# Third layer's edges: the last column of each half found by one-hot products in place of a gather

## The reference

```python
q = ((src @ q_w.T + q_b) * scaling).reshape(n, H, HD)
k = (src @ k_w.T).reshape(n, H, HD)
v = (src @ v_w.T).reshape(n, H, HD)
w = jnp.einsum('ehd,ehd->eh', q[e_dst], k[e_src])
mx = jax.ops.segment_max(w, e_dst, num_segments=n)
ex = jnp.exp(w - mx[e_dst])
den = jax.ops.segment_sum(ex, e_dst, num_segments=n)
attn_w = ex / (den[e_dst] + 1e-16)
agg = jax.ops.segment_sum(attn_w[:, :, None] * v[e_src], e_dst, num_segments=n)
x = _batchnorm(src + agg.reshape(n, D) @ out_w.T + out_b, g1, b1)
```

## Time and profile before

| | |
|---|---|
| time, median of 3 runs | 4790.94 us (4788.01 to 4792.92) |
| the profiled execution's own time | 4801.15 us |
| its span, first to last instruction | 4799.3 us |
| busy: DVE / POOL / ACT / PE | 3583.7 / 3313.6 / 2745.0 / 2121.5 us |
| mean granted TensorE clock | 0.736 |
| `layer2_edges` | about 2741 to 3752 us of the span |

### The profile page before, as it was taken

How to read it: one execution, slowest core, us unless ns; L and a number is a source line. 1 busy time by engine, 2 the same in 40 slices (tenths; PEclk the granted TensorE clock), 3 DMA queues, 4 the chain that set the end, 5 groups by cost and what they waited for, 6 DMA issues and landing times. The chain is left out here.

```text
span 4799.3 us, 60694 instructions
## 1 busy us (share of the span) xinstructions
PE 2121.5 (44%) x11977; PEld 1206.2 (25%) x11977; DVE 3583.7 (75%) x7007; ACT 2745.0 (57%) x6085; POOL 3313.6 (69%) x2937
## 2 busy tenths in 40 slices
PE   4499999999853000000000400000000458889995
PEld 3255554444422000000000200000000235555553
DVE  9365665555547899999997588888988657777776
ACT  0388888788722888888884322232222245655663
POOL 0488888888726777777772477777777337777774
PEclk9799999999976555555555755555555679999998
DMA  9655555555633577777674456666666323333332
GB/s 401 207 101 101 105 107 95 97 100 101 129 70 131 212 261 269 270 258 277 255 275 192 141 186 218 217 211 210 217 219 210 97 70 118 118 115 117 126 120 85
DMA packets 281953, 816.71 MB, mean 170 GB/s; under 512 B 62437, under 2 KB 177653, under 8 KB 269554
## 3 DMA queue, kind: packets, MB, share of 16 engines
q1 hardware_dynamic: 102828, 561.89, 31.0%
q0 software_dynamic: 169776, 248.56, 23.7%
q10 hardware_dynamic: 9238, 5.24, 0.5%
HBM read 366.96 MB, written 448.51 MB: 170 GB/s over the span
## 5 line engine op out<-in xcount | busy, mean ns | idle before, releaser
L643 POOL DMA_INDIRECT tab<-arena x560 | 952.4, 1701 | 210.3 <-issue 132.2
L1576 PE MATMUL psum<-ident,arena 128*128 128x128 f32 x15 | 3.7, 428 | 2145.9 <-DVEq L1604 2145.9
L773 PE MATMUL psum<-arena 128*128 128x512 bf16 (+1 forms) x4704 | 949.7, 357 | 0.0
L1948 POOL DMA_INDIRECT arena<-table,arena x784 | 748.1, 954 | 242.4 <-issue 238.5
L2448 POOL DMA_INDIRECT arena<-table,arena x622 | 630.1, 1013 | 191.3 <-issue 179.8
L1331 POOL DMA_INDIRECT arena<-table,arena x588 | 610.2, 1038 | 179.3 <-issue 172.3
L2530 PE MATMUL psum<-arena 128*128 (+1 forms) x4050 | 685.5, 332 | 90.6 <-DVE arena L2578 49.6
L773 PEld LDWEIGHTS psum<-arena 128*128 128x128 bf16 x4704 | 433.7, 99 | 473.6 <-issue 24.6
L1576 PEld LDWEIGHTS psum<-ident,arena 128*128 128x128 f32 x15 | 2.7, 214 | 2146.4 <-DVEq L1604 2146.2
L2530 PEld LDWEIGHTS psum<-arena 128*128 (+1 forms) x4050 | 402.0, 99 | 366.6 <-issue 115.8
L1379 ACT ACTIVATE arena<-arena 128x128 f32<-128x128 f32 x1344 | 408.8, 387 | 92.1 <-DVE arena L1498 88.5
(11 more groups left out here) (426 smaller groups left out, 5164.9 us busy)
## 6 DMA issues: line engine op xcount, KB each, us to landing
rows<-arena SPq DMA_DIRECT2D x56, 3808.0 KB
arena<-seg_rows SPq DMA_DIRECT2D x112, 896.0 KB, 7.1
rows<-arena SPq DMA_DIRECT2D x56, 1008.0 KB, 4.7
seg_rows<-arena SPq DMA_DIRECT2D x28, 1792.0 KB
rows<-arena SPq DMA_DIRECT2D x56, 896.0 KB, 3.9
arena<-table,arena POOLq DMA_INDIRECT x1994
arena<-src_lanes SPq DMA_DIRECT2D x56, 448.0 KB
tab<-arena POOLq DMA_INDIRECT x560
```

The costliest lines, as they stand in the source:

```text
L643: eng.indirect_dma_start(out=m.tabs[j], out_offset=bass.IndirectOffsetOnAxis(ap=idx[g][:, k:k + 1], axis=0), in_=rows[g][:, k, 0:D], in_of ...
L773: t = eng.matmul(ps[:, c, 0:w], part[n // 2 % PAIRS][:, n % 2, :], hot[n % HOTS][:, lo:lo + w], start=False, stop=False, skip_group_check= ...
L1948: eng.indirect_dma_start(out=kv[k][:, j, :], out_offset=None, in_=m.table2, in_offset=bass.IndirectOffsetOnAxis(ap=idx[k][:, j:j + 1], axi ...
```

## The change

For all but the first four halves, the 14th column is no longer gathered. `layer2_edges` loads `table2` into SBUF once and splits it into three bf16 parts (`part_cols`; the third lies in `xN`'s memory). For each half, SP loads keys to all partitions (index minus block start, for 25 blocks by 128 lanes), ScalarE turns them into the one-hot `hot` (Abs, then Relu), TensorE adds 25 blocks x 3 parts = 75 products of 256 columns into `found`, and ScalarE copies that to the place where the gather would have put it. To make room, queries have two buffers, the marks over all features one, and small tiles lie in weights already used. Since `xN` is overwritten, `layer2_nodes` adds the input on TensorE from `xT` by products with the identity, and VectorE only copies.

```diff
+HALVES = T // HALF
+SIX = 6
 def layer2_edges(nc, m, I):
-        q = [A(HALF, D) for _ in range(RING)]
+        q = [A(HALF, D) for _ in range(2)]
...
+        part_cols = [A(NB * 2 * D, dt=BF16) for _ in range(2)] + [m.xN[:, :, :].rearrange("p b f -> p (b f)").bitcast(BF16)]
+        hot = A(NB * P, dt=BF16)
+        KEYS = [(0, 13), (13, NB)]
+        found = m.psum[:, 2, 0:2 * D]
+        tab = [kv[3 - c].rearrange("p t f -> p (t f)")[:, 0:(b - a) * 2 * D] for c, (a, b) in enumerate(KEYS)]
-        all_keeps = [A(D, COLS) for _ in range(2)]
+        all_keeps = A(D, COLS)
...
             @block.sync
-                def turn(i, last):
+                def load_keys(at):
+                    for c, (a, b) in enumerate(KEYS):
+                        eng.dma_start(keys[c], m.keys2[at, a * P:b * P].rearrange("t l -> (t l)").partition_broadcast(P)).then_inc(keys_in, 16)
+                def turn(i, first, last):
                     for k in range(RING):
                         hold(eng, in_psum, i * RING + k + 1)
-                        if k == 0 or not last:
-                            load(i, k + RING - 1)
+                        if k < 2 or not last:
+                            load(i, k + 2)
+                        if (k >= 2 or not first) and (k < 1 or not last):
+                            hold(eng, apart, 2 * (nth(i, k) - 1))
+                            load_keys(bass.ds(i * RING + k + 3, 1))
                         hold(eng, sums_made, nth(i, k) + 2)
...
+                for c, (a, b) in enumerate(KEYS):
+                    eng.dma_start(tab[c].rearrange("p (b f) -> p b f", f=2 * D), m.table2.rearrange("(b p) f -> p b f", p=P)[:, a:b, :]).then_inc(tab_in[c], 16)
+                for k in range(2):
                     load(0, k)
+                eng.dma_start(lanes_found[0:HALVES, :], m.src_lanes[0:T, :].rearrange("(n t) l -> n t l", t=HALF)[:, HALF - 1, :]).then_inc(lanes_in, 16)
+                eng.wait_ge(keys_made, 1)
+                eng.dma_start(m.keys2, hot.bitcast(F16)[0:HALVES, :]).then_inc(keys_stored, 16)
...
             @block.gpsimd
-                with eng.Fori(0, LOOPS) as i:
+                gather(0, HALF)
+                with eng.Fori(1, LOOPS) as i:
+                    gather(i, HALF - 1)
+            @block.tensor
+            def _(eng):
+                def block_sums(g, n, first=False, last=False):
+                    for p, part in enumerate(part_cols):
+                        t = eng.matmul(found, hot[:, bass.ds(g * (SIX * P) + n * P, P)], part[:, bass.ds(g * (SIX * 2 * D) + n * 2 * D, 2 * D)],
+                                       start=(first and p == 0), stop=(last and n == SIX and p == 2))
+                    return t
+                eng.wait_ge(low_made, 2)
+                with eng.Fori(1, HALVES - RING + 1) as n:
+                    hold(eng, hot_made, n)
+                    block_sums(0, 0, first=True)
+                    with eng.Fori(0, (NB - 1) // SIX - 1) as g:
+                        for b in range(SIX):
+                            block_sums(g, 1 + b)
+                    for b in range(SIX):
+                        t = block_sums((NB - 1) // SIX - 1, 1 + b, last=True)
+                    t.then_inc(found_made, 1)
             @block.scalar
...
+                def one_hots(i, k):
+                    eng.wait_ge(keys_in, 32 * (nth(i, k) - 3))
+                    for c, (a, b) in enumerate(KEYS):
+                        eng.activation(hot[:, a * P:b * P], keys[c], ACT.Abs, bias=lane_ids[:, 0:1]).then_inc(apart, 1)
+                    eng.wait_ge(apart, 2 * (nth(i, k) - 3))
+                    eng.activation(hot, hot, ACT.Relu, bias=m.ones[:, 0:1], scale=-1.0).then_inc(hot_made, 1)
+                def keep_found(i, k):
+                    eng.wait_ge(found_made, nth(i, k) - 3)
+                    eng.wait_ge(free[k], i + 1)
+                    eng.activation(kv[k][:, HALF - 1, :], found, ACT.Copy).then_inc(found_in, 1)
...
                         hold(eng, scores_made, nth(i, k) + 2)
                         eng.activation(ex[h], gap[h], ACT.Exp, scale=-1.0).then_inc(exped, 1)
-                        stage_marks(k, edges(i, k + 2))
+                        if (k >= 3 or not first) and (k < 3 or not last):
+                            keep_found(*half(i, k + 1))
+                        stage_marks(k + 1, edges(i, k + 1))
                         if k + 1 < RING or not last:
                             keep_query(*half(i, k + 1), by_edge[:, HALF, :])
...
                         eng.activation(rows[h][:, :, MAX:R2], top[h][:, :, 1:COLS].rearrange("p a t -> p t a"), ACT.Copy).then_inc(filled, 1)
+                        if (k >= 2 or not first) and (k < 2 or not last):
+                            one_hots(*half(i, k + 2))
...
             @block.vector
                     elif step == 1:
-                        eng.wait_ge(landed[k], 16 * HALF * (i + 1))
+                        eng.wait_ge(landed[k], 16 * ((HALF - 1) * i + HALF))
+                        eng.wait_ge(found_in, nth(i, k) + 1)
...
+                eng.tensor_tensor(hot.bitcast(F16)[0:HALVES, :].rearrange("p (b l) -> p b l", l=P), spread(lanes_found[0:HALVES, :], 1, [HALVES, NB, P]),
+                                  spread(block_at[0:HALVES, :], 2, [HALVES, NB, P]), ALU.subtract).then_inc(keys_made, 1)
...
+                eng.wait_ge(low_made, 2)
+                for k in range(2, RING):
+                    eng.engine_nop().then_inc(free[k], 1)
                 for step in range(SCORES2):
                     score(0, 0, step)
...
 # layer2_nodes
-                        t = eng.transpose(ps[:, 6 + k % 2, n * P:(n + 1) * P], sT[:, b * P:(b + 1) * P], m.ident[:, :])
+                        to = ps[:, 6 + k % 2, n * P:(n + 1) * P]
+                        eng.matmul(to, sT[:, b * P:(b + 1) * P], m.ident[:, :], start=True, stop=False)
+                        t = eng.matmul(to, m.xT[:, b * P:(b + 1) * P], m.ident[:, :], start=False, stop=True)
...
-                    eng.tensor_tensor(y[:, b0:b1, :], ps[:, 6 + k % 2, 0:CHUNKS[k][1]].rearrange("p (b f) -> p b f", f=D), m.xN[:, b0:b1, :], ALU.add).then_inc(y_made, 1)
+                    eng.tensor_copy(y[:, b0:b1, :], ps[:, 6 + k % 2, 0:CHUNKS[k][1]].rearrange("p (b f) -> p b f", f=D)).then_inc(y_made, 1)
```

More of the change, by code:

```diff
@@ L1867 @@
 SUMS2 = OLD2 + HALF
+HALVES = T // HALF
+SIX = 6
+assert (NB - 1) % SIX == 0
 def layer2_edges(nc, m, I):
@@ L1884, in layer2_edges @@
         old = A(D + H2)
-        all_keeps = [A(D, COLS) for _ in range(2)]
+        all_keeps = A(D, COLS)
         keeps = [A(HALF) for _ in range(2)]
-        resets = [A(H2 * COLS + 1) for _ in range(2)]
+        resets = [used_up[:, 6 * H2 * COLS + h * (H2 * COLS + 1):6 * H2 * COLS + (h + 1) * (H2 * COLS + 1)] for h in range(2)]
         idx = [A(HALF, dt=I32) for _ in range(RING)]
         SUM, MAX = D, D + H2
-        q_first, q_in = sem("first_queries_landed"), [sem(f"queries_landed{k}") for k in range(RING)]
+        q_first, q_in = sem("first_queries_landed"), [sem(f"queries_landed{k}") for k in range(2)]
+        ids_made, lanes_in, keys_made, keys_stored = sem("block_ids_made"), sem("found_lanes_landed"), sem("keys_made"), sem("keys_stored")
+        keys_in, apart, hot_made = sem("keys_landed"), sem("keys_apart"), sem("one_hots_made")
+        found_made, found_in = sem("rows_found"), sem("found_rows_kept")
+        tab_in = [sem(f"table_landed{c}") for c in range(2)]
+        high_made, rest_made, mid_made, low_made = sem("high_parts"), sem("rests"), sem("middle_parts"), sem("low_parts")
         begun = sem("buffers_begun")
@@ L1946, in _ @@
                         hold(eng, free[k], i + 1)
-                        for j in range(HALF):
+                        for j in range(n):
                             eng.indirect_dma_start(out=kv[k][:, j, :], out_offset=None, in_=m.table2,
                                                    in_offset=bass.IndirectOffsetOnAxis(ap=idx[k][:, j:j + 1], axis=0)).then_inc(landed[k], 16)
+                gather(0, HALF)
[18 more added lines that the diff above has]
+                    t.then_inc(found_made, 1)
             @block.scalar
@@ L1955, in stage_marks @@
                                    spread(m.reset[:, at], 1, [P, H2, HALF]), ACT.Copy).then_inc(marks, 1)
-                    eng.activation(all_keeps[k % 2][:, :, 1:COLS], spread(m.keep[:, at], 1, [P, D, HALF]), ACT.Copy).then_inc(marks, 1)
+                    eng.activation(all_keeps[:, :, 1:COLS], spread(m.keep[:, at], 1, [P, D, HALF]), ACT.Copy).then_inc(marks, 1)
                 for k in range(RING):
@@ L1962, in keep_query @@
                     eng.activation(by_edge[:, 0, :], before, ACT.Copy).then_inc(last_kept, 1)
-                    eng.wait_ge(q_in[k], 16 * i + 16)
+                    eng.wait_ge(q_in[k % 2], 16 * (i * (RING // 2) + k // 2 + 1))
                     eng.wait_ge(last_kept, i * RING + k + 1)
```

(39 more changed lines are left out.)

40 lines of the change are left out of this document (30 added, 10 removed).

## The result

The changed kernel takes 5047.26 us, median of 4 runs (5032.8 to 5051.13), beside 4789.48 for the kernel before on the same chip (4 runs, 4786.49 to 4792.92). The ratio is 1.0532, 95% interval 1.051 to 1.0555: 5.3% slower. The forecast was 5201 with a range from 5000 to 5330; the direction and the place are right, the size is 154 us too large.

A forecast was written before the change was run, and what follows sets the result against it. POOL's gathers were taken to bound the third layer's edges, VectorE close behind. Start +16, first halves -2 and 52 slower halves +396 gave +410 us on the span; forecast median 5201 us, range 5000 to 5330.

The forecast's parts named there:

- What bounded the kernel, and what the gather was worth: Third layer's edges: POOL's gathers pace a half at 17.64 us; one gather fewer leaves VectorE's ring of 16.59.
- The new ring, without VectorE: Third layer's edges: found rows' copy 0.37, marks to state columns 4.49, one-hots 6.1, hand-overs 0.3, then TensorE's products.
- 11.26 + X: Cost in us of a half in the third layer's edges once X is over about 6; forecast 25.3.
- X: Time of TensorE's 75 products for a half in the third layer's edges, forecast at 14.0 us.
- Four register operations a block: TensorE's sequencer, loop over blocks: four address operations a block, 0.131 us apart; three turns take 11.4 us.
- The rival of the array: TensorE's array sets the products' pace, register operations hidden: X = 10.7, 22.0 us a half, 5030 us; 22%.
- The clock stays low: Rival: TensorE's product bursts never get the high clock: X = 16.0 + 0.3, 27.6 us a half, 5321 us; 15%.
- A reload in each ring: Rival: ScalarE reloads its table between exponentials and one-hots, +1.28 us in each of 52 halves: 5268 us; 5%.
- Products hidden: Rival: TensorE's products fit their gap, X at 6.0 or less, a half 16.95 us: 4769 us, faster; 4%.
- The start: Third layer's edges, up to the first exponential: table, lanes, keys and parts come first, 46.2 us for 30.3, +16.
- The first three halves: Halves at the start of the third layer's edges, forecast to gain 3 x 0.69 = 2.1 us.
- The nodes: Third layer's nodes: 25 more TensorE products run beside VectorE, whose additions become copies: 0 to +2 us, taken as 0.

The follow-up runs named there:

- Kernel 8: The kernel before with 13 gathers a half from the fifth on and nothing in the 14th's place: 4736.15 us, ratio 0.9898.
- kernel 1: The changed kernel with only the table's high part multiplied, 25 products a half: 6287.23 us on the first chip, 4765.66 us on another (ratio 0.9967).
- kernel 6: The changed kernel with one-hots made one half earlier and found rows in two PSUM banks, nothing left out: 4794.92 us, ratio 1.0018.
- kernel 9: The changed kernel with one-hots a half earlier, found rows' copy behind the state columns, blocks written out, one-hots' first 13 blocks released early: 4758.89 us, ratio 0.9954.
- kernel 2: The changed kernel with the loop's turns written out, no register arithmetic between products: 5990.85 us on the first chip, ratio 1.0256, distorted by pauses.
- kernel 3: The changed kernel with 82 (first 88) unread products behind each burst to keep the clock high: run again, 5030.9 us, ratio 1.0533.
- kernel 4: The changed kernel with turns written out and unread products added behind each burst (82 when run again): 4952.22 us, ratio 1.0364.

## Why the prediction came out as it did

- **What bounded the kernel, and what the gather was worth: right.** POOL's pace, with VectorE's ring close behind. Kernel 8 measures 48 us in all, where 1.05 us a half was forecast: 0.86 came.
- **The new ring, without VectorE: right, and shown.** The ring of `keep_found`, state columns, one-hots and products holds when taken apart at either end: fewer products (kernel 1) or one half of distance (kernel 6) and the wait is gone. Its ScalarE link was 10.9 us where 10.96 and hand-overs were forecast, and a half follows 11.26 + X: 22.4 by the measured X, 22.0 in the trace; what lies between is the 0.3 of hand-overs, which the two links as read from the timeline already hold.
- **X: the term that was mis-sized**, by 14.0 - 11.1 = 2.9 us. That the sequencer's loop ends the burst was right; how long its turn takes was not. The sum was 410 us on the span and 245 came: 170 too much in the 52 halves, of which 2.9 x 52 = 151 are X and the rest the hand-overs, and 5 too little at the start and in the first halves. "Four register operations a block" are three: 18 of them less at 0.131 us make 2.4 of the 2.9. The rest is in the turns too: three of them by the forecast's terms, each 18 x 0.131 + 0.7 = 3.06, would be 9.2, and they measured 8.6, mostly because the last turn takes only 2.6. The ends of the burst were right, 2.5 us where 2.6 was forecast. The four came from the fourth layer's block, with products of two widths; how the three are shared out among a block's addresses here the trace doesn't show. The variant that the forecast named, X = 11.6 and 5077, is 30 us from the measurement. That the result lies in the stated range owes something to the range's width, which took in the array's rival too: the forecast's own 410 us are 1.6 times the 257.8 measured.
- **The rival of the array, 5030**, is nearer in time than the forecast, 17 us off, and so the total can't choose between them. The experiments do, in part: without register operations a burst is still 10.4 us in the mean (kernel 9, and 10.8 in the pair of kernel 2), and without the low clock X is 11.1 (kernel 3). The sequencer is thus the longer of the two, by some 0.6 us in most bursts, and the array is close behind: while the clock is low the array takes 0.64 us a block and the sequencer runs ahead of it, and when the array is fast the sequencer holds it back (from 3218.5 on a block starts every 0.41 us, where 0.33 would do). Only both cures together bring it to 8.4 us, where the clock stays high (kernel 4). The forecast took one cause to be the limit and the other to be free.
- **The clock stays low: wrong.** It rises to 1.00 in each of the 52 bursts, 2.6 to 6.0 us after the first product. The Trainium skill (TensorE: Matmul & The Clock Gate, "HAM oscillation") says that bursts with waits between them lose the clock each time; the trace agrees, with 0.50 in the window of 3212 to 3216 and a low start in all 52 bursts. By itself it cost nothing that can be measured here, by kernel 3.
- **A reload in each ring: wrong.** The stage after has one ACT_TABLE_LOAD (the one at 2791.96) where the stage before had 13. The Trainium skill (ScalarE: Activation LUTs, "Table sets: the hidden batching unit") says that abs and relu are in every set, and this agrees.
- **Products hidden: wrong as the change stands**, and right for its idea: with X under 6 the forecast had 22 us less than before, and kernel 1 measures 15 less; at one half's distance and with an early release they are hidden (kernel 9), and the sign turns.
- **The start: +18.8 instead of +16.** Lanes, keys, rests, low parts and scan end 42.1 us into the stage, where the forecast had 40.9: 1.2 more. Another 1.28 is the table load in front of the first exponential, which the forecast left out, and 0.4 lies in the score steps and hand-overs, not divided further.
- **The first three halves: +0.4 instead of -2.1.** They took 16.6, 16.5 and 20.1 us. In the third VectorE stood still for 3.45 us up to 2840.22, before its product with the gathered rows; ScalarE, which waits for the same rows, goes on at the same moment. The forecast had POOL fill two buffers and said that being held then costs nothing. It filled one: its 15th gather lasts 17.4 us (16.7 to 17.5 in the eleven other profiles with this start), while VectorE makes the keys, the rests and the low parts without a pause (2764.76 to 2781.85), and so the 14 gathers of the fourth half were issued 17 us later than in the kernel before (to 2833.2 instead of 2815.8):

```profile
2765.24 17.42 POOL L1985 DMA_INDIRECT arena<-table,arena  x1 [0.30 <-issue]
```

  In the kernel before no gather of the stage's first 125 us takes more than 1.1 us. Why this one takes so long was not tested, and kernel 9, with the same long gather, has no such late half (16.6, 16.5, 16.6).
- **The nodes: above the 0 to +2 that was given.** Between POOL's first gathers of that stage and of the next lie 135.0 us after and 129.9 before in these two profiles, 131.8 to 134.6 in those of other kernels with the edit, and 129.8 in kernel 8, which is without it. The copies wait 4.5 us for TensorE instead of 2.0:

```profile
L2300 PE MATMUL psum<-ident,arena 128*128 128x128 f32 x50 | 10.7, 300 | 3.6 <-ACT arena L2356 3.6
L2301 PE MATMUL psum<-ident,xT 128*128 128x128 f32 x50 | 10.7, 298 | 0.0
L2453 DVE COPY arena<-psum 128x512 f32<-128x512 f32 (+1 forms) x7 | 4.4, 631 | 4.7 <-PE psum L2301 4.5
```

  The 25 transposes became accumulating f32 products, and each of these, and each identity product, stands in the trace twice: 100 records and 21.4 us of TensorE where there were 25 and 5.4. The forecast added 25. The nodes' edit alone was not run; kernel 8 beside the others puts it at 2 to 5 us, of which the copies' extra wait of 2.5 us is what the trace shows directly.

Summed: 18.8 + 0.4 + 226.1 instead of 16 - 2 + 396.

## What to carry over

When work moves into a ring of two engines, its length counts in full as soon as it is longer than the gap it is put into; look first at how many turns lie between producer and consumer, since one turn of distance was worth 235 us here, and the two cures that keep all 75 products 79 together. Count what an engine's sequencer does in the loop as a limit of its own, from the loop's own operands, and take the longer of it and the array at each clock level piece by piece: removing one of two nearly equal limits shows little or nothing, and is no proof that it was not one. Before trading a small saving (48 us), price what the trade needs at the start (19 us) and elsewhere (2 to 5). And read the clock of the very burst that is argued from: a window beside it can be at the other level.

## What was unexpected of the hardware

- On the first chip the kernel before took 5846.92 us (7 runs, 5830.3 to 5850.94) where the others took 4781 to 4789, while single instructions kept their durations. In the kernels profiled there ScalarE waits 15 to 30 us at a time at hand-overs from TensorE, in the fourth layer, which the change doesn't touch, as well. A group of kernel 1 on that chip; the same group of the kernel before (line 2516, 27 times) waited 139.4 in its profile, which is of the chip of the result:

```profile
L2625 ACT ACTIVATE arena<-psum 128x768 f32<-128x768 f32 x27 | 21.9, 810 | 795.3 <-PE psum L2639 795.3
```

  What makes these pauses was not found, and no profile of the kernel before was taken on that chip. The times on the other chips leave no room for such pauses.
- Behind gaps of only 2.0 to 2.1 us of idling, TensorE's clock had a low stretch in 25 of 51 bursts of kernel 3 (run again) and in 34 of 51 of kernel 4, and stayed high in the others; the first burst of either, after a long rest, is not counted. Idle times of 2.04 and of 2.12 us stand before bursts of either kind. What tells them apart was not tested.
- One gather at the stage's start takes 17.4 us in place of 0.95, while VectorE works without a pause (see the first three halves above). Its cause was not tested.
